# Moving the weight remainders to GpSimd and the last stage's additions into SBUF, in a fused mixer and mixture-of-experts kernel

## The reference, cut to what matters

```python
x = x + _layernorm(_L0_attn_ref(_layernorm(x), ...))      # x1 in the kernel
x = x + _layernorm(_L0_ffn_ref(_layernorm(x), ...))       # out

def _L0_attn_ref(x, ...):
    x = _lin(x, w1)
    x = _depthwise_conv(x, conv_w, conv_b)                # three taps
    x = jax.nn.silu(x)
    x_delta = jax.nn.softplus(_lin(x, dl_w, dl_b))
    A_bar = jnp.exp(-x_delta * _lin(x, A_w, A_b))
    h = jnp.cumsum(_lin(x, B_w, B_b) * jnp.cumprod(A_bar, axis=1), axis=1)
    ssm_out = _lin(h, C_w, C_b) + _lin(x, D_w, D_b)
    ...
```

## Time and profile before

| | before |
|---|---|
| median of 3 runs | 1121.13 us (1115.91 to 1122.24) |
| the profiled execution | 1116.39 us, span 1114.5 us |
| mean granted clock of PE | 0.978 |
| PE busy | 1022.9 us, 92% of the span |
| DVE busy | 801.9 us, 72% |
| ACT busy | 623.8 us, 56% |
| POOL busy | 286.8 us, 26% |

### The profile page before, as it was taken

One profiled execution on the slowest core, in us unless ns is written; L12 is line 12 of the kernel. 1 busy time (PEld: TensorE's weight loads), 2 busy tenths in 40 slices (PEclk: granted clock), 3 DMA queues, 4 the chain that ended last, 5 costly groups with the idle time before them and its releaser, 6 DMA issues.

```text
span 1114.5 us, 21512 instructions
## 1 busy us (share of the span) xinstructions
PE 1022.9 (92%) x7026; PEld 902.9 (81%) x7026; DVE 801.9 (72%) x2059; ACT 623.8 (56%) x1265; POOL 286.8 (26%) x303
## 2 busy tenths in 40 slices
PE   4889999989998999899999999999999999999930
PEld 2666677667676566799999999999999999999930
DVE  4997799888888857766666666666666666666645
ACT  6867868786876446344454444444544445445425
POOL 1133123453262273212121121211211212122134
PEclk9899999999999999999999999999999999999975
DMA  8656667886576588955563521735366822655149
GB/s 302 219 198 207 221 222 228 272 263 219 165 263 213 182 274 305 379 198 174 151 218 74 216 36 21 266 107 178 66 229 225 288 35 36 213 181 159 25 120 200
DMA packets 116518, 210.30 MB, mean 189 GB/s; under 512 B 9952, under 2 KB 75232, under 8 KB 116448
## 3 DMA queue, kind: packets, MB, share of 16 engines
q1 hardware_dynamic: 101040, 189.51, 49.0%
q0 software_dynamic: 15408, 19.93, 10.5%
HBM read 341.43 MB, written 86.02 MB: 384 GB/s over the span
## 4 chain that ended last, share of the span: by engine, by line
PE 75%; DVE 11%; DMA 4%; issue 3%; POOL 3%; ACT 2%; SPq 0%; DVEq 0%; ACTq 0%; POOLq 0%
PE bank L488 12%; PE bank L1461 10%; PE bank L1463 10%; PE bank L1462 10%; PE bank L1506 5%; PE bank L1508 5%; PE bank L1507 5%; PE bank L482 4%; PE bank L483 3%; PE bank L484 3%; POOL xs_scratch L1232 2%; DMA w_both<-w_split 1%; DVE h L925 1%; PE bank L1447 1%; PE bank L1479 1%
## 5 line engine op out<-in xcount | busy, mean ns | idle before, releaser
L1409 POOL DMA_INDIRECT acc_scratch<-cv,ids x71 | 111.5, 1571 | 504.1 <-DVE cv L1606 494.4
L1643 DVE TENSOR_SCALAR cv<-bank 128x256 f32<-128x256 f32 x284 | 120.5, 424 | 155.1 <-PE bank L1463 136.3
L1573 ACT ACTIVATE cv<-cv 128x256 f32<-128x256 f32 x284 | 118.4, 417 | 183.7 <-DVE cv L1643 183.7
L1461 PE MATMUL bank<-h_hi,w_both 128*128 128x256 f32 x640 | 178.0, 278 | 2.2 <-DMA w_both<-w_split 1.0
L1463 PE MATMUL bank<-h_hi,w_both 128*128 128x256 f32 x640 | 177.2, 277 | 0.0
L1462 PE MATMUL bank<-h_hi,w_both 128*128 128x256 f32 x640 | 177.2, 277 | 0.0
L1559 ACT ACTIVATE h_lo<-cv 128x256 fp32r<-128x256 f32 x256 | 106.8, 417 | 92.1 <-DVE cv L1646 92.1
L1646 DVE TENSOR_TENSOR cv<-bank,cv 128x256 f32<-128x256 f32 x284 | 120.3, 424 | 41.7 <-ACT cv L1573 34.6
L1461 PEld LDWEIGHTS bank<-h_hi,w_both 128*128 128x128 f32 x640 | 120.2, 188 | 3.1 <-issue 2.3
L1463 PEld LDWEIGHTS bank<-h_hi,w_both 128*128 128x128 f32 x640 | 120.3, 188 | 0.0
L1462 PEld LDWEIGHTS bank<-h_hi,w_both 128*128 128x128 f32 x640 | 120.3, 188 | 0.0
(11 more groups left out here) (293 smaller groups left out, 2819.1 us busy)
## 6 DMA issues: line engine op xcount, KB each, us to landing
w_both<-w_split SPq DMA_DIRECT2D x155, 776.0 KB
single_ring<-w_split SPq DMA_DIRECT2D x14, 3880.0 KB
w_split<-e_both SPq DMA_DIRECT2D x128, 256.0 KB, 4.0
e_both<-w_e SPq DMA_DIRECT2D x64, 384.0 KB, 3.5
h_lo<-w_split SPq DMA_DIRECT2D x31, 776.0 KB
xs_lo<-w_split SPq DMA_DIRECT2D x31, 776.0 KB
single_ring<-w_split SPq DMA_DIRECT2D x14, 1552.0 KB
w_split<-e_both SPq DMA_DIRECT2D x64, 264.0 KB, 3.7
```

The lines of the kernel that those rows point to most:

```text
L1461: nc.tensor.matmul(out, gu_hi[f][:, cols], xg_hi[:, par, c, :], start=c == 0, stop=False)
L1643: nc.vector.tensor_scalar(half, gate_ps, CLIP, -CLIP, ALU.min, ALU.max).then_inc(clipped, 1)
```

## The change

- The remainders `p0` to `p4` of the mixer's weights move from DVE to POOL, which runs them right after `m0/0 m1/0` and ahead of `m0/1`.
- ACT's `p3/0 w2/0` move from behind `c0/0 c1/0` to behind `r0/0 r1/0`, ahead of `c2/0 c3/0`; DVE's `w2/0` moves behind `r0/0 r1/0` too.
- All eight chunks of x1 are loaded into SBUF. Chunks 0 to 3 are moved after SP's turns 1 to 4 as before, chunks 4 to 7 after the turns 31 to 34, into the places of g, `w_sh` and n2. No chunk is copied to the output in DRAM.
- The even chunks no longer go out as adding DMAs. POOL adds x1 to chunks 0, 2 and 5 itself with a 128x1024 addition, DVE to 1, 3, 4, 6 and 7. POOL's order is root 0 to 2, add 0, root 3 and 4, add 2, root 5 to 7, add 5; DVE's is m0 m1 m2 a1 m3 m4 a3 m5 m6 m7 a4 a6 a7.
- The last chunk is added and stored in two halves, and ACT tells of each half. SP stores in the order 0 1 2 3 4 6 7 5, every store a plain one.

```diff
+POOL_ADDS, DVE_ADDS = (0, 2, 5), (1, 3, 4, 6, 7)
 LEAD, BODY, REPEATS = 5, 4, 6
+PAST = LEAD + BODY * REPEATS + 1
 CW = 4 * P + D
...
+        n2_flat = n2[:, :, :, :].rearrange("p h t d -> p (h t d)")
+        x1 += [by_tile(flat(g[:, :, :])), by_tile(w_sh[:, 0:TC * D]), by_tile(n2_flat[:, 0:TC * D]), by_tile(n2_flat[:, TC * D:2 * TC * D])]
...
 "scalar":
-                "p0/0 N0/0 N1/0 t0/0 t1/0 t2/0 p1/0 t3/0 p2/0 u0/0 w0/0 w1/0 u1/0 u2/0 u3/0 c0/0 c1/0 p3/0 w2/0 S0/0 S1/0 r0/0 r1/0 "
...
+                "p0/0 N0/0 N1/0 t0/0 t1/0 t2/0 p1/0 t3/0 p2/0 u0/0 w0/0 w1/0 u1/0 u2/0 u3/0 c0/0 c1/0 S0/0 S1/0 r0/0 r1/0 p3/0 w2/0 "
...
 "vector":
-                "m0/0 m1/0 k/0 p0/0 p1/0 w0/0 p2/0 w1/0 c0/0 c1/0 p3/0 w2/0 r0/0 r1/0 c2/0 c3/0 m0/1 w3/0 dt0/0 p4/0 da0/0 dt1/0 "
...
+                "m0/0 m1/0 k/0 w0/0 w1/0 c0/0 c1/0 r0/0 r1/0 w2/0 c2/0 c3/0 m0/1 w3/0 dt0/0 da0/0 dt1/0 r2/0 da1/0 ac0/0 bx0/0 w4/0 "
...
 "gpsimd":
-                "m0/0 m1/0 m0/1 lo0/0 lo1/0 lo2/0 lo3/0 tab/0 lo4/0 m1/1 lo5/0 d0.5/0 lo6/0 lo7/0 d0.6/0 d1.5/0 d1.6/0 lo0/1 lo1/1 "
...
+                "m0/0 m1/0 p0/0 p1/0 p2/0 p3/0 p4/0 m0/1 lo0/0 lo1/0 lo2/0 lo3/0 tab/0 lo4/0 m1/1 lo5/0 d0.5/0 lo6/0 lo7/0 d0.6/0 "
...
-            def split_low(b, n):
-                at, src, chunks = weights[n]
-                cols = slice(at, at + chunks * src.shape[1])
-                dve.wait_ge(w_hi_ready, n + 1)
-                nc.vector.tensor_tensor(w_lo[:, cols], raw_w[:, cols], w_hi[:, cols], ALU.subtract).then_inc(w_lo_ready, 1)
...
+            def split_low(b, n):
+                at, src, chunks = weights[n]
+                cols = slice(at, at + chunks * src.shape[1])
+                pool.wait_ge(w_hi_ready, n + 1)
+                nc.gpsimd.tensor_tensor(w_lo[:, cols], raw_w[:, cols], w_hi[:, cols], ALU.subtract).then_inc(w_lo_ready, 1)
...
             def move_x1(c):
-                if c % 2 == 0:
-                    sp.dma_start(token_rows(out)[c, :, :, :], token_rows(x1_dram)[c, :, :, :]).then_inc(x1_moved, 16)
-                else:
-                    sp.dma_start(x1[c // 2], token_rows(x1_dram)[c, :, :, :]).then_inc(x1_moved, 16)
+                sp.dma_start(x1[c], token_rows(x1_dram)[c, :, :, :]).then_inc(x1_moved, 16)
+
+            def turn_and_move(i, n):
+                turn(i, n)
+                if n > PAST and NC // 2 + n - PAST - 1 < NC:
+                    if n == PAST + 1:
+                        sp.wait_ge(down_done, before(0, PAST, steps_at) + FC)
+                    move_x1(NC // 2 + n - PAST - 1)
 
             free(sp, "x1")
             move_x1(0)
             free(sp, "tables")
-            for c in range(1, NC):
+            for c in range(1, NC // 2):
                 turn(0, c + 1)
                 move_x1(c)
-            slots(sp, turn, NC + 1)
+            slots(sp, turn_and_move, NC // 2 + 1)
...
-            for c in range(1, NC, 2):
-                sp.wait_ge(sum_ready, c // 2 + 1)
-                sp.dma_start(token_rows(out)[c, :, :, :], acc[c]).then_inc(sum_stored, 16)
-            sp.wait_ge(sum_stored, 16 * (NC // 2))
-            sp.wait_ge(out_added, 16 * (NC // 2))
+            for c in (0, 1, 2, 3, 4, 6, 7, 5):
+                if c in POOL_ADDS:
+                    sp.wait_ge(pool_sums, POOL_ADDS.index(c) + 1)
+                elif c < NC - 1:
+                    sp.wait_ge(sum_ready, DVE_ADDS.index(c) + 1)
+                for k, part in enumerate((slice(0, TC // 2), slice(TC // 2, TC)) if c == NC - 1 else (slice(0, TC),)):
+                    if c == NC - 1:
+                        sp.wait_ge(sum_ready, len(DVE_ADDS) + k)
+                    sp.dma_start(token_rows(out)[c][:, part, :], acc[c][:, part, :]).then_inc(sum_stored, 16)
+            sp.wait_ge(sum_stored, 16 * (NC + 1))
...
-            def add_out(c):
-                if c == 0:
-                    pool.wait_ge(x1_moved, 16 * NC)
+            def add_x1(c):
                 pool.wait_ge(normed, c + 1)
-                nc.gpsimd.dma_start(token_rows(out)[c, :, :, :], acc[c], accum_op=ALU.add).then_inc(out_added, 16)
-
-            root(0)
-            root(1)
-            for c in range(2, NC):
+                nc.gpsimd.tensor_tensor(acc[c], acc[c], x1[c], ALU.add).then_inc(pool_sums, 1)
+
+            pool.wait_ge(x1_moved, 16 * NC)
+            for c in range(NC):
                 root(c)
-                if c % 2 == 0:
-                    add_out(c - 2)
-            add_out(NC - 2)
+                if c in (2, 4):
+                    add_x1(c - 2)
+            add_x1(5)
...
-                i.then_inc(normed, 1)
+                    if t == TC - 1 or (c == NC - 1 and t == TC // 2 - 1):
+                        i.then_inc(normed, 1)
...
-                dve.sem_inc(seen, 1)
...
             def add_x1(c):
-                if c == 1:
+                if c == DVE_ADDS[0]:
                     dve.wait_ge(x1_moved, 16 * NC)
-                dve.wait_ge(normed, c + 1)
-                nc.vector.tensor_tensor(acc[c], acc[c], x1[c // 2], ALU.add).then_inc(sum_ready, 1)
+                for k, part in enumerate((slice(0, TC // 2), slice(TC // 2, TC)) if c == NC - 1 else (slice(0, TC),)):
+                    dve.wait_ge(normed, c + 1 + k)
+                    nc.vector.tensor_tensor(acc[c][:, part, :], acc[c][:, part, :], x1[c][:, part, :], ALU.add).then_inc(sum_ready, 1)
 
             for c in range(NC):
                 moments_of(c)
-                if c % 2 == 1 and c > 1:
-                    add_x1(c - 2)
-            add_x1(NC - 1)
+                if c in (2, 4):
+                    add_x1(c - 1)
+            for c in (4, 6, 7):
+                add_x1(c)
```

More of the change, by code:

```diff
@@ L1077, in fullest @@
                 i.then_inc(star_ready, 1)
-            run("vector", {"x": first_lo, "star": fullest, "m": x_moments, "p": split_low, "k": bias_sum, "c": conv_sides, "r": xs_remainder, "dt": delta_unit, "da": da_unit,
+            run("vector", {"x": first_lo, "star": fullest, "m": x_moments, "k": bias_sum, "c": conv_sides, "r": xs_remainder, "dt": delta_unit, "da": da_unit,
                            "ac": acum_unit, "bx": bx_unit, "h": h_unit, "d": d_stage, "w": w_stage,
@@ L1247, in _ @@
             pool.wait_ge(start_made, 1)
-            run("gpsimd", {"m": x_root, "tab": make_tables, "lo": h_remainder, "d": d_stage})
+            run("gpsimd", {"m": x_root, "p": split_low, "tab": make_tables, "lo": h_remainder, "d": d_stage})
             all_groups()
@@ L1288, in experts @@
     rooted, rs_ready, normed = sem("f_rooted"), sem("f_rs_ready"), sem("f_normed")
-    x1_moved, out_added = sem("x1_moved"), sem("out_added")
+    x1_moved, pool_sums = sem("x1_moved"), sem("pool_sums")
     sum_ready, sum_stored = sem("sum_ready"), sem("sum_stored")
```

## The result

The changed kernel takes 1127.19 us (median of 7 runs, 1124.77 to 1131.72), the kernel before 1119.42 on the same chip (7 runs, 1115.91 to 1122.24). The ratio is 1.0074, interval [1.006, 1.0089]: 7.8 us slower. A second comparison, on another chip, gave the ratio 1.0071 [1.0043, 1.0098]. The forecast was +11.8 us, to 1132.9, with a range from 1119 to 1138.

A forecast was written before the change was run, and what follows sets the result against it. PE, holding 75% of the chain, was taken as the bound, the change mattering only where PE waits or has ended. Start +3.8, experts 0 and last stage +8.0 made +11.8 us, to 1132.9 against the median, range 1119 to 1138.

The forecast's parts named there:

- The port: Start and last stage: POOL and DVE both reading SBUF run one after the other; +11.8 us with it, +1.9 if shared freely.
- the signs named: POOL's p3 about 2.5 us, w2 2.6, dt0 near 42, a1 and a3 over 3, last addition 5 to 9 us later.
- both races: Last stage: POOL's add 0 and add 2 each start 0.1 us ahead of DVE's a1 and a3 and block them.
- Start: +3.8 forecast: Mixer start: POOL's p3 and p4 block DVE's w2 and a c2 side tap; dt0 comes 3.8 us late, passed to the end.
- They cost nothing: Mixer start: p0, p1 and p2 on POOL, from 11.6 to about 21.4 while DVE has little to do, cost 0.
- rival 4: Mixer start: PE, idle about 4.0 us for dt0, loses its full clock; about 2 us more, 1134.9; chance 0.08.
- Experts and the rest of the mixer: 0 forecast: Experts: later x1 moves fit SP's idle time, 0 (from -1 to +1); later mixer: start's delay passes whole.
- Last stage: +8.0 forecast: Last stage: last addition 8.6 us later, 0.45 for store order, 1.1 back for landing; 8.0, with 6.8 to 9.1.
- the walk: Last stage, new order followed step by step: last addition ends at 1114.3 instead of 1105.7, 8.6 us later.
- 1.1 for landing and lost 0.45 for the queue: Behind the last addition: last store lands in 5.1 us instead of 6.2 (-1.1); chunk 5's store queues behind chunk 7's (+0.45).
- Rival 3: Last stage: adding DMAs hold the end and nothing blocks; -3.9, with PE's earlier start -4.6, 1116.5; chance 0.07.
- rival 1: Last stage: DVE wins both races, a1 and a3 run unblocked; stage +4.4, sum +8.2, 1129.3; chance 0.23.

The follow-up runs named there:

- first three: Kernel before with only p0, p1 and p2 moved to POOL; one execution: first side tap at 23.01, dt0 at 35.68, 12.67 between them.
- additions all on DVE: Changed kernel with all eight last-stage additions on DVE, none on POOL, stores in order 0 to 7; ratio to before 0.9992 [0.9972, 1.0012].
- start alone: Kernel before with only the change's mixer edits (p0 to p4 on POOL, p3 and w2 later); ratio to before 1.0011 [0.9986, 1.0036].
- the best: Changed kernel with only p0 to p2 on POOL, p3 and w2 reordered, all last-stage additions on DVE; ratios to before 0.9944 and 0.9978.
- order alone: Kernel before with r0 and r1 ahead of p3 and w2 on DVE and ACT, subtractions staying on DVE; one execution, 14.06 us to dt0.
- one adding DMA less: Kernel before with chunk 6 added by DVE and stored plainly, chunk 7 in halves, later x1 moves; one execution, last stage 28.10 us.
- the two parts run alone: Kernel before with only the change's mixer edits, 1.0011; changed kernel with the start of before, 1.0024 [1.0001, 1.0048]; both ratios to before.

## Why the prediction was right or wrong

**The port (right).** Of the signs named, these came: p3 of 2.39 near 29 with w2 at 2.51, a1 and a3 over 3 us, the last addition 6.9 us later. One sign did not come: dt0 was to be near 42 and came at 39.51, at the very edge of what I had named as wrong (before 39.5); the next paragraph says why. POOL won both races, as forecast, with 0.35 and 0.2 us in hand. Where I had only scans and products to go by, side taps turned out to be held up too (1.67). The rule of the Trainium skill ("SBUF — State Buffer", section "Who interferes with whom") is borne out for DVE instructions with two inputs in SBUF: here 2.51, 1.67, 3.08 and 3.22 us instead of 0.95, 0.75 and 1.22. The one-input operation of 1.93 is a `tensor_scalar`, and the same section counts `tensor_scalar` among the instructions that can enter a mode with both ports and then contend, if its operands allow it; that the mode was on no trace shows.

**Start: +3.8 forecast, +3.5 to dt0 from the first tap, and +3.6 to bx0, but by another sum.** Two things that I had left out nearly cancel.

The first is a gain. The step that failed is "They cost nothing" for p0 to p2: that their move gives something was put at nothing. The 0.7 us on PE's way from the first side tap to its first unit came as forecast (5.74 before, 5.04 after). But the first side tap itself comes 2.0 us earlier, and dt0 with it: +1.49, not +3.8. Part of it hangs on p0. Before, DVE's p0 held the port against POOL's small product of the second half of x. Timelines of before, DVE, POOL and PE:

```profile
10.34 1.22 DVE L839 TENSOR_TENSOR w_both<-xnt,w_both 128x1024 fp32r<-128x1024 f32 x1
...
10.61 1.00 POOL L1193 TENSOR_TENSOR nm<-mv,rs 128x4 f32<-128x4 f32 x1
...
10.97 1.97 PE L499 MATMUL bank<-ident,x_in 128*128 128x128 f32 x8 [10.97 <-ACT x_in L678]
13.78 1.97 PE L499 MATMUL bank<-ident,x_in 128*128 128x128 f32 x8 [0.84 <-ACT x_in L678]
```

The product took 1.00 instead of 0.20, ending when p0 did, and PE's transposes of the second half came late. The changed kernel, POOL and PE:

```profile
10.36 0.20 POOL L1190 TENSOR_TENSOR nm<-mv,rs 128x4 f32<-128x4 f32 x1
10.51 2.35 POOL L1213 TENSOR_TENSOR w_both<-xnt,w_both 128x1024 fp32r<-128x1024 f32 x1
...
10.82 3.94 PE L502 MATMUL bank<-ident,x_in 128*128 128x128 f32 x16 [10.82 <-ACT x_in L681]
```

With p0 behind it on POOL the product takes 0.20, and all 16 transposes run in one go, ending at 14.76 instead of 15.75. So moving p0 to POOL frees POOL. That is 1.0 of the 2.0; the other 1.0 lies in the products behind them, which take 7.46 instead of 8.44. In the trace of before the first three steps from one of these 16 products to the next are 0.85 us, the fourth is 0.56 and the rest are 0.43; in the changed kernel only the first is 0.85. As 0.85 is twice 0.43, I read the long steps as those at half the clock. They end where the trace's record of the full clock begins, at 18.37 before and at 15.41 after (ahead of that the trace has no record of the clock). Over all traces that record begins at 17.1 to 19.3 in the five traces with the pause of 0.8 between the transposes and at 13.8 to 16.7 in the nine without it; that the pause is the cause is not shown. Over all traces the first side tap is at 24.56 to 25.72 in the five with p0 on DVE and at 22.77 to 23.93 in the nine with it on POOL. The run with only the first three moved keeps this gain and pays nothing for it: dt0 comes at 35.68, against 38.02 and 37.22 before.

The second is a loss, rival 4, to which I had given 0.08. I had forecast the idle time well (4.0; it was 4.3), and called it too short to lose the clock. The table separates it cleanly: the five traces with 3.9 us or more of idle have PE at 1.2 GHz behind it and 6.76 to 8.00 from dt0 to bx0; the nine others, with 1.7 or less, have 5.91 to 5.94 and the full clock. The price is 0.8 to 2.1 us, as forecast for that rival (2), and it follows how long the clock stays low once PE has started again: 3.2 us of it cost 0.8, 4.7 cost 1.5 and 5.8 cost 2.1 (additions all on DVE, start alone, changed). That the gain and this loss nearly cancel, so that +3.6 stands beside the +3.8 of the forecast, is luck.

That a late start reaches the end is shown by the timed pairs that differ in it. In three comparisons a kernel with the slow start stood beside one with the start of the best: 5.9, 4.2 and 9.7 us apart (medians), of which the last stage, by the traces, makes 0.4, 1.3 and 6.3. What is left, 5.5, 2.9 and 3.4 us, has an uncertainty of 2 to 3 us each, and bx0 differs by 4.4, 5.0 and 5.6. So most of the delay is not taken back by slack.

**Experts and the rest of the mixer: 0 forecast, +3.7 between the two profiled executions, for the most part not shown to be the change.** The experts took 610.38 us in the first trace of before and 612.32 in the second, 612.40 in the changed kernel. Sorted by the places of x1's moves, the five traces with the early ones have 610.4 to 612.4 (mean 611.8), the nine with the late ones 611.9 to 613.9 (mean 612.9). So a cost of about 1 us of the later moves is possible; it doesn't show as waits for weights, which were 0.6 and 0.5 us against 1.0 of the earlier trace rows. The mixer behind bx0 scatters from 414.8 to 432.4 over the traces, with the start changed or not, so 1.7 can't be read there. The 414.8 is the first trace of before, which was a quick one: it alone has no stretch at 1.2 GHz between 35 and 1070 us, while all others have some before the experts begin.

**Last stage: +8.0 forecast, +2.2 measured.** This is the mis-sized term. Up to the last addition the walk holds: +6.9 against 8.6, since the 1024-wide addition takes POOL 2.34, not 2.5, a chunk's statistics 2.00, not 2.09 (the `seen` increments are gone), and ACT 2.0 a chunk, not 2.1. Root 7, too, was held up as I wrote: 1.91. But behind the last addition I had taken back 1.1 for landing and lost 0.45 for the queue; it took back 4.7. It comes in two parts. The last store is issued 0.4 later behind its addition, but lands in 3.0 us, below both of my ends (3.96, which was a load's, and 6.2); from its issue to SP's end signal are 3.5 us instead of 6.35, 2.9 less. And before, the end waited for something other than that store. In the records of the trace its last packet ends at 1111.56 and SP gives its end signal at 1112.08, but GpSimd gives its own only at 1114.04. In the changed kernel these are 1123.44, 1123.98 and 1124.01. So 1.9 us of the end were GpSimd's. I had seen 2.6 us behind the landing and counted them as fixed. GpSimd's signal follows the adding DMA: in the five traces that end with one of chunk 6 (before twice, start alone, order alone, first three) it comes 3.82 to 3.85 us after the last adding packet. In the run with one adding DMA less that would be 1119.16 + 3.83 = 1122.99, ahead of SP's 1123.78, and there GpSimd signals at 1123.81, with SP.

The same traces say more of this. GpSimd's last work of its own is a DRAIN instruction, which stands in the trace's records and in no view shown here. In the six traces with adding DMAs in the last stage it ends 3.78 to 3.80 us after the last adding packet (at 1122.93 in the run with one less). In the eight without, it ends 3.80 to 3.81 us after GpSimd's last addition or root. So the wait isn't particular to adding DMAs, any late work of GpSimd has it: in the changed kernel add 5 ends at 1118.90 and the DRAIN at 1122.70, only 1.3 us ahead of SP's signal.

Rival 3 had named the adding DMAs as what holds the end. It was right on that, but not on its condition that nothing blocks. The rest of the 4.7, 0.3, is between GpSimd's signal and the span's end.

**The sum.** On the traces, +3.6 (again: +4.6) and +2.2 make 5.8 to 6.8 of the 7.8 us, just below the interval (6.7 to 10) or at its lower end. The forecast of 11.8 was too high by the last stage, and by nothing else that can be told apart. By the number alone rival 1 (+8.2) would fit better, but what it rests on, that DVE wins the races, did not happen. Where the other 1 to 2 us are, if they are real, stays open, with the experts as one candidate; the two parts run alone give 1.0011 and 1.0024, whose sum of +3.9 us has an interval of some 4 either way. The start of the best kernel together with the last stage that has one adding DMA less was not tried; by the table it would save 1.5 us more than the best kernel.

## What to carry to other kernels

Before you hand an elementwise operation to GpSimd, list what VectorE does in that stretch: here the move was free where VectorE was idle or took one of its inputs from PSUM, and where both engines read SBUF together the pair ran one after the other, with GpSimd taking twice the time (2.34 us for 1.22). Work that leaves VectorE can give GpSimd's own small operations back their time, so look on both sides. And when you price the end of a kernel, follow each engine's last signal, not the last store alone: here GpSimd's came 3.8 us after its last work or its last adding DMA, and held the end whenever that was later than the last store's signal.

## What the runs showed of the hardware

- A 128x4 operation with a constant and one SBUF input on VectorE took 1.93 us beside a GpSimd addition of 2.35 (normally 0.17), while a 128x2 aggregation beside the same addition kept its 0.38. In the second trace of the changed kernel an operation of the same shape took 2.31 beside p0.
- What reads PSUM was not held up. Over the 14 traces, VectorE's 128x512 operations with one input in PSUM and one in SBUF (`dt`, `da`, `bx`) took 0.72 to 0.75 us in each of the 146 cases in which they ran beside a GpSimd subtraction for 0.6 us or more, and 0.75 alone; scans, with two inputs in SBUF, took 1.7 to 2.4 instead of 1.22 to 1.28. bn_stats took 0.40 to 0.43, its usual length, in 70 cases (in 56 of them its input was in SBUF).
- GpSimd is held up in the same way: the 128x4 root took 1.91 instead of 1.01 beside a 1024-wide addition on VectorE, and the 128x4 product 1.00 instead of 0.20.
- GpSimd gave its end signal 3.83 us after the last packet of the last adding DMA, in five traces within 0.02, and its closing DRAIN ended 3.8 us after its last work in the eight traces without such a DMA. With a plain store whose last packet came 4.1 us after the adding one (1119.16, 1123.24) this cost nothing; with one 1.4 us after it (1110.21, 1111.56) it cost 1.9 us.
- 512 KB stored with no adding DMA beside it landed in 3.0 us, 256 KB in 2.3; beside adding DMAs 5.4 to 6.2 and 3.9.
- TensorE lost its full clock over idle times of 3.9 to 4.8 us at this place, and kept it over 1.7 us. Short stretches at 1.2 GHz also come and go later in the mixer, at changing places, in every trace but the first of before.
